# A longer addition on GpSimd between runs of four indirect transfers, in a five-stage mixture-of-experts and recurrence kernel

## What is computed

```python
x = x + 0.5 * moe_gelu(layernorm(x))      # top 2 of 8 experts, output normalised
x = x + state_space(layernorm(x))
x = x + 0.5 * moe_gelu(layernorm(x))
x = x + 0.5 * moe_swiglu(layernorm(x))    # top 2 of 8 experts
x = x + receptance(layernorm(x))
x = x + 0.5 * moe_swiglu(layernorm(x))
```

## Time and profile before

| | us |
|---|---|
| Timed runs (3): lowest, median, highest | 1335.67, 1336.54, 1336.85 |
| Span of the profiled execution, first to last instruction | 1697.2 |
| GpSimd busy in the span | 751.0 |
| TensorE busy in the span | 1114.7 |

### The profile page before, as it was taken

How to read it: one execution, slowest core, us unless ns; L and a number is a source line. 1 busy time by engine, 2 the same in 40 slices (tenths; PEclk the granted TensorE clock), 3 DMA queues, 4 the chain that set the end, 5 groups by cost and what they waited for, 6 DMA issues and landing times. The chain is left out here.

```text
span 1697.2 us, 28236 instructions
## 1 busy us (share of the span) xinstructions
PE 1114.7 (66%) x6835; PEld 926.2 (55%) x6836; DVE 765.2 (45%) x2839; ACT 553.5 (33%) x1653; POOL 751.0 (44%) x802
## 2 busy tenths in 40 slices
PE   2376888437656699867477548289799734768482
PEld 2375888434346588757376547234344334657372
DVE  5221324158671133544146313269979762335132
ACT  1133546247413255533032113134343301223131
POOL 3634263521054625545715552255645456442522
PEclk9787999678966799978688769589999955879696
DMA  8544567310023345544354436100000003445363
GB/s 251 169 143 138 183 197 245 109 41 1 0 81 111 130 165 196 181 133 139 109 198 159 140 118 205 53 0 1 1 0 0 0 29 127 165 152 203 117 208 106
DMA packets 198792, 199.71 MB, mean 118 GB/s; under 512 B 22212, under 2 KB 140310, under 8 KB 198678
## 3 DMA queue, kind: packets, MB, share of 16 engines
q1 hardware_dynamic: 123138, 136.22, 23.5%
q0 software_dynamic: 16384, 33.59, 6.6%
q10 hardware_dynamic: 59156, 28.57, 5.9%
HBM read 52.44 MB, written 49.02 MB: 60 GB/s over the span
## 5 line engine op out<-in xcount | busy, mean ns | idle before, releaser
L611 PE MATMUL gelu_hb<-gelu_xsT,gelu_weights 128*128 128x128 f32 x2208 | 340.1, 298 | 65.5 <-issue 61.3
L611 PEld LDWEIGHTS gelu_hb<-gelu_xsT,gelu_weights 128*128 128x128 f32 x2208 | 308.7, 213 | 75.4 <-issue 73.5
L708 ACT ACTIVATE gelu_hid<-gelu_hb,gelu_weights 128x128 f32<-128x128 f32 x736 | 208.8, 374 | 238.6 <-remote 127.1
L1190 POOL DMA_INDIRECT slots_x<-gelu_xn,gelu_index x176 | 172.4, 980 | 203.6 <-DVE gelu_index L921 154.2
L622 PE MATMUL gelu_ob<-w,gelu_hid 128*128 x1472 | 220.0, 292 | 43.8 <-issue 41.5
L961 DVE TENSOR_TENSOR gelu_ys<-gelu_ob,bias 128x128 f32<-128x128 f32 x184 | 51.7, 291 | 392.4 <-PE gelu_ob L622 176.1
L622 PEld LDWEIGHTS gelu_ob<-w,gelu_hid 128*128 128x128 f32 x1472 | 198.7, 206 | 51.4 <-issue 51.1
L611 PE MATMUL swiglu_hb<-swiglu_xsT,swiglu_weights 128*128 128x128 f32 x736 | 114.8, 302 | 27.3 <-issue 27.2
L611 PEld LDWEIGHTS swiglu_hb<-swiglu_xsT,swiglu_weights 128*128 128x128 f32 x736 | 104.2, 217 | 29.0 <-issue 29.0
L952 DVE TENSOR_TENSOR gelu_hid<-gelu_sil,gelu_hb 128x256 f32<-128x256 f32 x92 | 38.4, 419 | 151.9 <-ACT gelu_sil L712 82.0
L952 DVE TENSOR_TENSOR swiglu_hid<-swiglu_sil,swiglu_hb 128x256 f32<-128x256 f32 x92 | 38.5, 419 | 149.3 <-ACT swiglu_sil L712 72.8
(11 more groups left out here) (375 smaller groups left out, 1997.1 us busy)
## 6 DMA issues: line engine op xcount, KB each, us to landing
gelu_weights<-w SPq DMA_DIRECT2D x184, 258.0 KB
gelu_weights<-s SPq DMA_DIRECT2D x92, 256.0 KB
swiglu_weights<-s SPq DMA_DIRECT2D x92, 256.0 KB
gelu_xs<-slots_x SPq DMA_DIRECT2D x69, 256.0 KB
slots_y<-gelu_ys ACTq DMA_DIRECT2D x138, 128.0 KB
swiglu_xs<-slots_x SPq DMA_DIRECT2D x23, 256.0 KB
slots_y<-swiglu_ys ACTq DMA_DIRECT2D x46, 128.0 KB
slots_x<-zeros SPq DMA_DIRECT2D x2, 1984.0 KB
```

What stands on the lines that cost most here:

```text
L611: last = pe.matmul(hb[j][:, c * P:(c + 1) * P], weights[:, j, c * P:(c + 1) * P], xsT[j // SET][:, j % SET, :], start=True, stop=True)
L708: last = act.activation(hid[:, j % RING, c * P:(c + 1) * P], hb[j][:, c * P:(c + 1) * P], ACT.Gelu, bias=weights[:, j, FF + c:FF + c + 1])
L1190: pool.indirect_dma_start(slots_x[:, :], bass.IndirectOffsetOnAxis(index[p][:, k, g:g + 1], 0), tokens[p][:, g, :], None).then_inc(sent[p] ...
```

## The change

The addition between runs of four transfers has 128x512 elements in place of 128x4. It reads two tiles of 128x128 elements, each four times over, and `pause` grows from 4 to 512 elements per partition. Number, place and waits of the additions stay as they were, and so does the useful addition `shift`.

```diff
-        pause = L.sb("pause", [P, SUB])
+        pause = L.sb("pause", [P, SUB, D])
...
-                rests.step(pool.tensor_tensor(pause[:, :], res["ones"][:, 0:SUB], res["neg_half"][:, 0:SUB], ALU.add))
+                over = lambda t: t.rearrange("p (a d) -> p a d", a=1).broadcast_to([P, SUB, D])
+                rests.step(pool.tensor_tensor(pause[:, :, :], over(res["ones"][:, :]), over(res["post_b"][:, :]), ALU.add))
                 rests.settle()
```

## The result

| | kernel before | kernel after |
|---|---|---|
| Median of the timed runs, us (4 each, side by side) | 1336.11 (1334.81 to 1336.85) | 1383.79 (1382.35 to 1384.70) |
| Ratio, with its 95% interval | | 1.0351 (1.0334 to 1.0368) |

The change costs 47.7 us. 1396.0 was predicted, that is 59.9 us of cost; the sign, the range and the mechanism hold, the size is 12 us too high.

The account below looks back on a forecast made before the run. The prediction took GpSimd to bound the third mixture and take turns with TensorE in the joint one. Of 81 additions 56 counted, at 1.07 us each 59.9 us, added to 1336.5: 1396 us, range 1345 to 1425.

Parts of the forecast that it names:

- The choice that the timed runs hold few stalls: TensorE's stalls during transfer bursts, the whole 360 us between span and median, belong to the profiled execution; timed ones have few.
- item 4: Tails of the first and joint mixtures: 3 of 4 additions in fetch(2), 6 of 8 in fetch(5) and fetch(6) count.
- item 3: Middle of the joint mixture, from the end of fetch(1) to send(4): 5 of 7 additions count.
- item 2: Late part of the joint mixture, send(5) and then fetch(3), fetch(4), send(6): TensorE waits, all 16 additions count.
- item 5: Rest of the third mixture, send(2) to fetch(2): 16 additions in a row without a wait, 11 counted.
- first wait of the third mixture: send(1) of the third mixture: TensorE is ready near 1439, set 5 can run at 1442, so all 5 additions count.
- cross-check: The same reckoning of the kernel before gives about 1300 us for the whole; 35 us up to 1336.5 left open.
- The shared port: A long addition on GpSimd can hold up VectorE: priced at 0 to 8 us, 0 in the sum, at most 86.
- B: Rival: additions mostly hidden, transfers faster without the profiler; 10 to 31 count, 1347 to 1370 us, or no change; chance 0.18.
- A: Main case: the path is GpSimd's, 45 to 75 additions on it; 1396 us, 1376 to 1425; chance 0.65.
- C: Rival: faster, the longer gap frees TensorE and gives back 0.55 of any timed stall, deciding from 109 us; chance 0.12.
- D: Rival: the addition is worse than its row through contention, all 81 count; 1423 us and more with VectorE; chance 0.05.

Follow-up runs that it names:

- experiment 1: The kernel before, unchanged, profiled once more: 1337.34 us, ratio 1.0005.
- Experiments 11 and 12: 11: changed kernel with its addition cut to 128x352 elements, 1365.99 us; 12: kernel before with a write of zeros over 128x1024 for the short addition, 1360.64 us.

## Why the prediction was right, and where its size was off

**The choice that the timed runs hold few stalls.** Right for the chips on which the change was timed, for a wrong reason. That the stalls belong "to the profiled execution alone" is refuted: on one chip the timed runs have them too, and on the others the profiled execution has none of this kind. The 17 us per burst tested nothing: they were had by dividing the 360 us by 21 bursts. That the timed runs are free of stalls followed from 1336.54 against 1697.2 alone. The prediction called this its weakest step. That it did no harm is in part luck: on the other chip parts of the change make the kernel faster.

**The cost of one addition.** 1.07 us was right: 1274 - 216 and 1278 - 212 ns are 1.06 and 1.07. In all 85.7 us against 86.4.

**How many lie on the path.** The terms of the sum beside what the starts of the 14 rows give, in us of delay. One slip of the prediction changes nothing in its sum: outside its five items there are 15 additions and not 22 (81 less 15, 16, 7, 12 and 16).

| stretch | predicted | measured | from |
|---|---|---|---|
| first mixture, send(1) | 5.3 | 5.0 | -0.39 to +4.64 |
| first mixture, the rest (item 4 and hidden ones) | 3.2 | 5.0 | to +9.61 |
| joint, send(1) | 5.3 | 5.7 | +9.67 to +15.33 |
| joint, to send(5) (item 3 and hidden ones) | 5.3 | 3.7 | to +19.02 |
| joint, send(5) up to fetch(5) (item 2, and the one addition of send(7)) | 17.1 | 16.8 | to +35.85 |
| joint, tail (item 4) | 6.4 | 0.9 | to +36.70 |
| third, send(1) | 5.3 | 2.1 | +36.76 to +38.81 |
| third, the rest (item 5) | 11.8 | 6.3 | to +45.1 (spans) |

The sums are 59.9 and, with -0.39 at the start and twice 0.06 between mixtures, 45.1. Item 2 was sized best: 16.8 us, of 18.2 for the 17 additions of the stretch. The first mixture's rest was too small, item 3 a little too large, and three terms much too large. The *tail of the joint mixture* was counted at 6 of 8 additions; its wait for stores at 810.73 went from 10.14 to 2.84 us and took nearly all. The *first wait of the third mixture* was counted in full; 2.05 of 5.3 us shows. And *item 5* failed at its words "in a row without a wait by my reckoning": GpSimd waited 4.91 us at 1234.03 and 10.11 at 1294.88, and the additions reduced this to 0.35 and 2.82.

What was mis-sized behind these is the pace of the products. The prediction had 5.8 us for a set of four swiglu tiles, so 133 us for TensorE's 23 sets against 161 of GpSimd's transfers, and took GpSimd for the bound. SP's queue in the kernel before (experiment 1), the load of the third set and the last load of a set, 20 sets later:

```profile
1157.56 0.41 SPq L499 DMA_DIRECT2D swiglu_xs<-slots_x  x1
...
1297.73 0.39 SPq L499 DMA_DIRECT2D swiglu_xs<-slots_x  x1
```

The pace is 140.2 / 20 = 7.0 us per set, and 23 sets take 161 us, as long as GpSimd's transfers. It is not GpSimd that sets this pace. From 1160 to 1305 us TensorE is busy for 130.4 of 145 us, at a granted clock of 1.00:

```profile
1160.00:1305.00 145.00, 130.38 (x1117) 125.28 (x1116) 79.01 (x302) 53.85 (x147) 93.09 (x110) 1.00 0.81 264
```

SP waits for GpSimd's transfers for 0.3 us in it. So GpSimd is not the bound throughout this mixture; the two take turns here too. 5.8 was the pace of two tiles in an undisturbed stretch; what else TensorE and VectorE do between sets was left out. The gelu sets were taken too fast as well: in the first mixture of the same trace 18 sets take the 153.7 us from 88.2 to 241.9, 8.5 us each and not 7.6. A slower pace of the products means more waits of GpSimd, and waits are what hides an addition. It probably is also what the cross-check left "open" (1300 us for 1336.5), but no run takes these 35 us apart.

**The shared port.** Priced at 0 to 8 us and 0 in the sum. Experiments 11 and 12 give 5.4 us at 0.94 us of length, within the bounds, and far from the 86 us that the prediction gave as what it could be at most. Most of what VectorE loses is not on the path: in these two experiments it was busy for 22.1 us more with the read. The 45.1 us include it. If it costs as much at 1.27 us, which was not measured by itself, the additions' own part is 40, and the reckoning of the path was 20 us too high and not 15. Then the two errors partly cancel, and that is luck.

**The rivals.** B (mostly hidden) supposed transfers that are faster without the profiler; against that speaks that the profiled run takes no longer than the other three (1383.24 us among 1382.35 to 1384.70). Its time for 31 additions is 1370, and the measured 1384 lies between it and A. C is refuted on the chips where the whole change ran; its effect is real on another. D is excluded: 41.9 of the 85.7 us went into waits. Of the signs named, the 1275 ns and the unchanged counts came, and 2.63 us for the 2.54; the span did not test anything, since the two profiles came from executions of different kind.

**The fastest version found.** The kernel without the additions, 0.5 to 0.7% below the one before. It was not tried on the chip with the stalls, where a gap between transfers is worth more than it costs.

## What to carry to other kernels

Work added to an engine in a hand-written list costs what is left after that engine's own waits are filled: add up those waits stretch by stretch in a trace whose span agrees with the timed runs, since what was added cost 20, 56 and 69% of its length as they were used up. If the profile's span and the timed median differ by 27%, don't repair the trace in the head; take the pace of a whole stretch and not of its best tile, and get a second trace before trusting a wait in it. And a sign measured on one chip need not hold on another: the same lines cost 3.5% here, while parts of them gave 1.4 to 4.0% there.

## What the runs showed of the hardware that was not expected

On one chip the kernel before takes 1703 to 1711 us in all seven runs, on the others 1332 to 1342. The trace ahead of the prediction has nearly that length (1697.2 us) and the same stalls; that it comes from the same chip is not on record. It shows TensorE in order of time in the stall of fetch(2), each line with an idle time that nothing in the profile ends:

```profile
319.60 0.37 PE L611 MATMUL gelu_hb<-gelu_xsT,gelu_weights 128*128 128x128 f32 x1 [1.74 <-issue]
321.73 1.09 PE L611 MATMUL gelu_hb<-gelu_xsT,gelu_weights 128*128 128x128 f32 x3 [1.75 <-issue]
324.54 0.37 PE L611 MATMUL gelu_hb<-gelu_xsT,gelu_weights 128*128 128x128 f32 x1 [1.73 <-issue]
```

The idle times are 1.7 us each, while GpSimd's transfers run at their usual 1.26 us. VectorE and ScalarE slow down alike (10 and 14 instructions in those 34 us, against 68 and 73 in experiment 1). That three engines stop together with no wait on record points to how they get their next instruction, but no run tests it. What in the chip does this, and whether it stays with the chip or with its condition at that hour, is open. A gap of 1.27 us in place of 0.21 after each four transfers brought back 26 us with 15 gaps, 44 with 16, 47 with 21 and 70 with 44.
